# Moving the sums of the convolution weights from VectorE to GpSimd in the opening of a graph-network kernel

## The reference, cut to what matters

```python
h  = relu(layernorm(x))
c  = relu(bn1(h @ conv1_w))                      # 1x1 convolution
xc = relu(bn2(conv1d(c, conv2_w, 17 taps)) + h)  # the 17-tap convolution
s  = h @ w_se.T + b_se
A  = exp(-|s_n - s_m|^2) * adj
nm = A @ relu(h @ w_msg.T + b_msg)
r, z, n = gates(xc, nm, h)                       # GRU cell
x  = x + (1 - z) * n + z * h
x  = x + adj @ (relu(layernorm(x)) @ W1) + bias
```

## Time and profile before

| what | us |
|---|---|
| median of three runs | 340.39 (340.17 to 340.74) |
| the profiled execution, own time | 340.39 |
| its span in the trace | 338.6 |
| PE busy | 324.5 (96%) |
| DVE busy | 265.0 (78%) |
| ACT busy | 221.5 (65%) |
| POOL busy | 145.1 (43%) |

### The profile page before, as it was taken

One profiled execution on the slowest core, in us unless ns is written; L12 is line 12 of the kernel. 1 busy time (PEld: TensorE's weight loads), 2 busy tenths in 40 slices (PEclk: granted clock), 3 DMA queues, 4 the chain that ended last, 5 costly groups with the idle time before them and its releaser, 6 DMA issues.

```text
span 338.6 us, 6261 instructions
## 1 busy us (share of the span) xinstructions
PE 324.5 (96%) x2162; PEld 290.6 (86%) x2162; DVE 265.0 (78%) x746; ACT 221.5 (65%) x434; POOL 145.1 (43%) x128
## 2 busy tenths in 40 slices
PE   7798998979999999999999999999999999999995
PEld 4587785869989898899989998899988998899894
DVE  5797989999679977898688986899686885684474
ACT  2898655877676785677775786676776764444353
POOL 7010315027922297036932198025940199028014
PEclk9999999999999999999999999999999999999999
DMA  7902000001210031001210031001200000000003
GB/s 228 351 12 87 1 2 0 1 2 63 95 33 2 9 111 68 2 1 60 97 34 0 3 124 61 2 0 35 74 21 0 2 31 33 0 3 0 3 0 125
DMA packets 7951, 15.02 MB, mean 44 GB/s; under 512 B 1008, under 2 KB 1648, under 8 KB 7792
## 3 DMA queue, kind: packets, MB, share of 16 engines
q1 hardware_dynamic: 7776, 14.62, 12.6%
q10 hardware_dynamic: 144, 0.01, 0.0%
HBM read 10.43 MB, written 4.19 MB: 43 GB/s over the span
## 4 chain that ended last, share of the span: by engine, by line
PE 62%; DVE 17%; ACT 8%; issue 7%; POOL 3%; DMA 1%; POOLq 0%; DVEq 0%; ACTq 0%
PE pQ L326 5%; PE pQ L328 5%; PE pQ L327 5%; PE pP L328 4%; PE pP L326 4%; PE pP L327 4%; PE pNR L326 4%; PE pNR L327 4%; PE pNR L328 4%; PE pF L444 3%; DVE st L1020 2%; ACT work L784 2%; PE pZ L504 2%; PE pI L326 2%; PE pI L328 2%
## 5 line engine op out<-in xcount | busy, mean ns | idle before, releaser
L1408 POOL TENSOR_TENSOR rs<-ve,neg_half 128x4 f32<-128x4 f32 x15 | 15.6, 1039 | 90.6 <-DVE ve L1178 90.6
L326 PE MATMUL pP<-cx_hi,conv_hi 128*128 128x256 f32 (+1 forms) x179 | 53.8, 301 | 0.0
L328 PE MATMUL pP<-cx_hi,conv_lo 128*128 128x256 f32 (+1 forms) x179 | 51.6, 288 | 0.0
L327 PE MATMUL pP<-cx_lo,conv_hi 128*128 128x256 f32 (+1 forms) x179 | 51.4, 287 | 0.0
L1403 POOL TENSOR_TENSOR rs<-ve,neg_half 128x8 f32<-128x8 f32 (+1 forms) x9 | 15.5, 1718 | 71.4 <-DVE ve L1027 71.4
L326 PE MATMUL pQ<-cx_hi,conv_hi 128*128 128x256 f32 (+1 forms) x139 | 41.5, 299 | 1.0 <-DVE cx_lo L1102 1.0
L327 PE MATMUL pQ<-cx_lo,conv_hi 128*128 128x256 f32 (+1 forms) x139 | 39.7, 286 | 0.0
L328 PE MATMUL pQ<-cx_hi,conv_lo 128*128 128x256 f32 (+1 forms) x139 | 39.7, 285 | 0.0
L784 ACT ACTIVATE work<-work,nb,rs 128x128 f32<-128x128 f32 x60 | 24.8, 483 | 17.4 <-DVE nb L1182 16.9
L326 PEld LDWEIGHTS pP<-cx_hi,conv_hi 128*128 128x128 f32 x179 | 33.9, 190 | 0.6
L327 PEld LDWEIGHTS pP<-cx_lo,conv_hi 128*128 128x128 f32 x179 | 33.9, 189 | 0.5
(11 more groups left out here) (281 smaller groups left out, 985.4 us busy)
## 6 DMA issues: line engine op xcount, KB each, us to landing
x_ring<-x_in SPq DMA_DIRECT2D x16, 256.0 KB, 2.9
adj_ring<-adj_in SPq DMA_DIRECT2D x16, 256.0 KB, 3.0
out<-x_ring SPq DMA_DIRECT2D x15, 256.0 KB, 2.0
work<-conv_in SPq DMA_DIRECT2D x1, 1088.0 KB, 8.2
x_ring<-gate_in SPq DMA_DIRECT2D x1, 576.0 KB, 7.9
out<-x_ring SPq DMA_DIRECT2D x2, 128.0 KB, 1.8
early<-early_in SPq DMA_DIRECT2D x1, 129.5 KB, 5.5
late<-late_in SPq DMA_DIRECT2D x1, 128.0 KB, 8.0
```

The lines of the kernel that those rows point to most:

```text
L326: pe.matmul(acc, w_hi, m_hi, start=start, stop=False)
L327: pe.matmul(acc, w_hi, m_lo, start=False, stop=False)
L328: return pe.matmul(acc, w_lo, m_hi, start=False, stop=stop)
L1408: pool.tensor_tensor(rs2[g % 2][:], ve2[g % 2][:], neg_half[:, 0:GG], ALU.pow).then_inc(rs2_set, 1)
```

## The change

`sum_halves` leaves DVE's opening, where it stood between `conv_lo_out(0, 0)` and `conv_out(0, 1)`, and is written for POOL with the same two additions. On POOL it stands behind `scale1([2, 3])` and a new wait for `pair_set` to reach 2, which is set by `pair_rows(1)` on DVE, and ahead of the first `pre`. It also waits for the load of the weights and for `wsum_set` at 1.

```diff
@@ DVE
-            def sum_halves():
-                dve.tensor_tensor(conv[:, taps(8, M12)], conv[:, taps(8, A0)], conv[:, taps(8, A2)], ALU.add)\
-                   .then_inc(wsum_set, 1)
-                dve.wait_ge(wsum_set, 2)
-                dve.tensor_tensor(conv[:, taps(4, M22)], conv[:, taps(4, M12)], conv[:, taps(4, M32)], ALU.add)\
-                   .then_inc(wsum_set, 1)
-
...
                 conv_lo_out(0, 0)
-                sum_halves()
                 conv_out(0, 1)
@@ POOL
+            def sum_halves():
+                pool.wait_ge(conv_loaded, 16)
+                pool.wait_ge(wsum_set, 1)
+                pool.tensor_tensor(conv[:, taps(8, M12)], conv[:, taps(8, A0)], conv[:, taps(8, A2)], ALU.add)\
+                    .then_inc(wsum_set, 1)
+                pool.wait_ge(wsum_set, 2)
+                pool.tensor_tensor(conv[:, taps(4, M22)], conv[:, taps(4, M12)], conv[:, taps(4, M32)], ALU.add)\
+                    .then_inc(wsum_set, 1)
+
             def opening():
                 scale1([2, 3])
+                pool.wait_ge(pair_set, 2)
+                sum_halves()
                 pool.wait_ge(pair_set, 4)
```

## The result

| | before | changed |
|---|---|---|
| median of five runs each | 340.74 us (340.17 to 341.38) | 338.31 us (338.19 to 339.45) |
| ratio, 95% interval | | 0.9937 (0.9913 to 0.9960) |
| the profiled execution, its span | 340.39, 338.6 | 339.45, 337.7 |

The change is faster, by 0.4 to 0.9%. The profiled execution of the changed kernel is the slowest of its five, and the reason for that turned out to be a part of the story of its own. So the path first.

What follows compares the result with a forecast made beforehand. PE was taken to bound the steps, DVE's queue the opening. 340.39 us less 1.85 for the removed additions plus 0 for those on POOL gave 338.54, forecast 338.5 us, range 338.1 to 339.7.

Steps and rivals of the forecast that it cites:

- What bounded the kernel: PE bounds the steps; in the opening, 46 to 59 us, PE waits for DVE's queue, where the additions stand.
- the long wait of ACT: ACT's 3.09 us of idle time for the additions, claimed to be worth nothing except through conv_out(0, 1) on DVE.
- What was removed: The two additions on DVE, 46.11 to 47.97 us: gain between 1.79 and 1.86 us, taken as 1.85.
- The next bound: Ahead of conv_out(0, 1), PE's last matmul into pP ends at 45.99, leaving 0.12 us before 46.11.
- PE's cover at `o_turn(0)`: PE's wait for DVE ahead of 59.41, claimed to fall from 1.43 us to 0.2 or less.
- What was added: Two additions on POOL from 25.30 to near 29.2 us, together 3.7 to 3.85 us in idle time: cost 0.
- The precedent of the earlier trace: Step 1: one DVE instruction is held behind POOL's first addition, the next stands until the second is done (1.82 us).
- the 0.4 us that the prediction counted: Cover left at PE's odd taps: split_lo_first(3) would end at 36.7 us, while PE comes to them at 37.12.
- The third rival: Slower: DVE stands behind both POOL additions through the SBUF port; 341.9 us at twice their price; chance 0.06.
- the turning point of 1.6 times POOL's price: The additions would have to take 6.1 us for right_rows(1) to be 3.8 us late and the gain gone.
- No change: Second rival: another wait in step 1 takes back the 1.85 us, giving 340.2 to 340.6 us; chance 0.10.
- a part lost: First rival: the second half of pP comes late, 0.6 us lost, 339.1 us; chance 0.14 for 338.9 to 339.7.

Runs made afterwards that it cites:

- The run with one addition: Changed kernel with only the 1024-column addition on GpSimd, the 512-column one staying on VectorE: median 339.13 us, ratio 0.9957 to the kernel before.
- the doubled run: Changed kernel with three more 512-column additions to a spare buffer on GpSimd in the opening: median 340.32 us, 339.69 at full clock, ratio 0.9982 to before.
- the stub: Kernel before with spare matmuls in PE's wait, both additions on DVE cut to 8 columns, and a POOL memset: median 339.90 us, ratio 0.9975 to before.
- early pre: Changed kernel with GpSimd's pre(1, 4) and pre(1, 5) moved ahead and split_lo(1, 0) moved into DVE's wait: median 337.06 us, ratio 0.9896 to before.

## Why the prediction was right

**What bounded the kernel.** Right: the additions were on the path of DVE's queue, and the long wait of ACT for them was worth nothing. The run with one addition gave back the share of the other, 0.61 us for 0.60.

**What was removed.** 1.85 us were forecast; 1.86 are seen at `o_turn(0)` (43.27 - 41.41), 1.94 by the times at full clock. The next bound, PE's last matmul into pP, stayed 0.1 us behind as worked out; with `split_lo(1, 0)` out of the way it shows as DVE's wait of 0.20 us. PE's cover at `o_turn(0)` was to be 0.2 or less and is 0.23.

**What was added.** POOL 2.37 and 1.39 us, for 2.4 and 1.28; ended at 29.0, for 29.2; line 997 at 39.3. The precedent of the earlier trace rows held: the first held instruction gets in between the two additions, the second stands until the later one is done. `right_rows(1)` was to be 1.5 us late and was 1.27; of that 0.2 were to be left at 32.69, and nothing was. Cost 0, as forecast, but with less to spare than the 0.4 us that the prediction counted: PE's distance matmul behind `right_rows(1)` had a cover of 0.17 (the doubled run made `right_rows(1)` 1.38 us later and this matmul 1.21). From that run it can start 0.84 us behind the start of `right_rows(1)`; on the prediction's own 29.8 it would have been 0.05 us late for its 30.59 in the kernel before. That nothing at all was lost there is in part luck.

**The third rival's arithmetic was wrong**, in two steps that the doubled run shows. DVE does not stand until all of POOL's additions are over: it is held once for each and gets in between, so `right_rows(1)` was 1.38 us later than in the changed kernel and not 3.8. And the cover was counted at the odd taps (37.12 in the earlier trace rows), while the first to wait is PE's distance matmul at 30.6, directly behind `right_rows(1)`; the prediction had named this reader and then left it out of the point of decision. There is next to no cover there, and so 1.31 of the 1.38 us reached `o_turn(0)`. The two errors go in opposite directions, and the turning point of 1.6 times POOL's price has nothing to stand on; at twice the price the kernel was still not slower than before.

**The size of the result** was met at full clock, 338.3 for 338.5. What the prediction did not see is that one profile does not show what the median is made of. It took the granted clock of 1.00 in all slices for a property of the kernel, while 54 of 70 executions have a mean below that, with a median 1 us higher. So the two medians, 340.74 and 338.31, differ by 2.4 us and those of the second set by 1.7, beside 1.9 at the full clock. That four of the first five executions of the new kernel had the full clock is luck: the second median, 339.5, is only just inside the range of 338.1 to 339.7, which had been widened for another reason.

**No change, a part lost:** neither occurred. Behind `o_turn(0)` the steps took as long as before, apart from the stretch with the low clock (PE's lead of 0.84 us at 92 us is 0.9 at the end).

## What to carry to other kernels

Moving work to an engine that is slower at it pays when that work stands in the queue of the engine on the path and the slower one has nothing to do there; price it by the queue's start-to-start time, and look for the next bound behind it. GpSimd's additions beside DVE instructions with two SBUF inputs cost DVE a hold for each of them, so put them beside DVE work that reads PSUM or has a wait behind it; a hold that is only pushed on comes back at the next such instruction, and moving GpSimd's preparations out of the way, together with one DVE instruction, was worth 1.2 us more. And before a profile's clock is taken as given, look at the spread of the times: executions of one program can differ by more than the change under study.

## What the runs showed of the hardware

- TensorE's granted clock fell to half (1.2 GHz) for 3 to 4 us near 71 us in the three profiles with a mean of 0.993 or 0.994, all of the changed order. A mean below 0.998 is rare when PE is given spare matmuls in its wait ahead (0 of 6, 2 of 12, 1 of 6, and 2 of 12 with the stub, against 54 of 70 and 8 of 17 without; but 0 of 4 with early pre without them). Such executions are 1 us longer at the median in the kernel before (341.23 against 340.25) and 1.8 in the new (340.08 against 338.31), though the shortest of the kernel before (340.07) lose nothing. With PE's wait lengthened to 2.12 us it came in 12 of 12.
- One instruction can take two lengths in two executions of a program: at 19 us, where DVE and POOL start within 0.2 us of one another, POOL's power takes 1.67 or 2.77 us, and with 2.77 the opening behind it is 0.8 us later. That the two engines change places at the SBUF port is the likely cause, not a tested one.
- A held DVE instruction got in between two additions of POOL each time that one was due, when the second waited for the first's semaphore (0.63 us for 0.46 at 27.22, line 1110) and also when it waited for none (the doubled run, at 27.8 and 31.8 us, where POOL's additions are 0.2 and 0.5 us longer for it). No row stood longer than one addition, the longest being 2.64 us behind 1024 columns.
- POOL's power on 8 columns does not hold DVE's two-input instructions (0.68 us for line 1133, 512 columns, inside it in all 12 profiles, as at 53 us in the kernel before); at 19 us it is, on the reading above, itself held by them. The Trainium skill, "SBUF — State Buffer", section "Who interferes with whom", says that whoever issues first has the pair for the whole instruction; by that the DVE row would have been longer, and here the measurement decides. POOL and then DVE in the changed kernel near 50 us (start, duration, engine, line; the bracket is the wait ahead):

```profile
50.47 1.65 POOL L1395 TENSOR_TENSOR rs<-ve,neg_half 128x8 f32<-128x8 f32 x1 [7.03 <-DVE ve L1027]
```

DVE inside that power, at its usual length:

```profile
50.90 0.68 DVE L1133 TENSOR_TENSOR conv_lo<-work,conv_hi 128x512 fp32r<-128x512 f32 x1
```

- A memset on POOL, which reads nothing, stretched a DVE instruction with one SBUF input and an SBUF output from 1.11 to 2.15 us (four of them). The same page says that `tensor_scalar` can run in a mode that uses both port pairs and then contends with GpSimd; the trace agrees.
